# Attention kernel: two PSUM banks for the score tiles and four for the maxima's chunks, in place of three and three

## What is computed

```python
energy = jnp.einsum('bhqd,bhkd->bhqk', q, k)
att = jax.nn.softmax(energy, axis=-1) / D ** 0.5
out = jnp.einsum('bhqk,bhkd->bhqd', att, v)
```

## Time and profile before

| | |
|---|---|
| median of three runs | 2861.51 us (2854.57 to 2863.14) |
| the profiled execution | 2858.09 us, its span 2856.3 us |
| mean granted TensorE clock of the span | 0.976 of full speed |
| matmuls of scores (L385), count and mean | 2048, 419 ns |
| matmuls of chunks (L371), count and mean | 2048, 424 ns |
| exponentials (L463), count and mean | 2048, 607 ns |
| maxima (L502), count and mean | 2048, 681 ns |

### The profile page before, as it was taken

The page is one execution under the profiler, slowest core; times in us unless marked ns, Lnnn a source line. Parts: engine busy times, 40 slices in busy tenths (PEclk is TensorE's granted clock), DMA queues, the critical chain, the costliest instruction groups (busy, mean ns, idle before and its releaser), DMA issues. The chain is left out here.

```text
span 2856.3 us, 61816 instructions
## 1 busy us (share of the span) xinstructions
PE 2659.4 (93%) x22219; PEld 1494.5 (52%) x22273; DVE 2204.9 (77%) x4467; ACT 1844.1 (65%) x3329; POOL 1962.6 (69%) x1571
## 2 busy tenths in 40 slices
PE   7899899999999999999759998999899899959998
PEld 5655466554765547555325554554455455524444
DVE  5778678776888768877677768776878688749998
ACT  4366555665556645566456677667766776658997
POOL 0389724896269952799438987998789799965442
PEclk9999999999999999999979999999999999989999
DMA  6122443223432415223222314322332222252001
GB/s 229 39 58 63 149 123 101 58 69 133 140 94 57 121 70 166 70 62 95 74 78 60 77 32 115 80 57 45 102 79 60 69 76 58 50 205 97 33 29 38
DMA packets 102196, 243.54 MB, mean 85 GB/s; under 512 B 18828, under 2 KB 25108, under 8 KB 101016
## 3 DMA queue, kind: packets, MB, share of 16 engines
q1 hardware_dynamic: 100120, 233.49, 28.9%
q0 software_dynamic: 1792, 6.33, 0.6%
HBM read 99.15 MB, written 38.88 MB: 48 GB/s over the span
## 5 line engine op out<-in xcount | busy, mean ns | idle before, releaser
L502 DVE TENSOR_REDUCE a_mxs<-ps 128x1 f32<-128x512 f32 x2048 | 1268.5, 681 | 256.7 <-PE ps L371 254.3
L463 ACT ACTIVATE a_p<-ps 128x512 f32<-128x512 f32 x2048 | 1042.6, 607 | 202.5 <-PE ps L385 192.2
L342 POOL TENSOR_TENSOR a_sum<-a_p 128x512 f32<-128x512 f32 x768 | 985.3, 1292 | 127.3 <-PE ps L403 104.9
L371 PE MATMUL ps<-a_k,a_q 96*128 96x512 f32 x2048 | 855.0, 424 | 27.9 <-DVE a_mxs L502 24.3
L385 PE MATMUL ps<-a_q,a_k 98*128 98x512 f32 x2048 | 810.4, 419 | 18.6 <-ACT a_p L463 12.4
L347 POOL TENSOR_TENSOR a_sum<-a_sum,a_p 128x512 f32<-128x512 f32 x512 | 663.5, 1296 | 40.1
L403 PE MATMUL ps<-a_sum,a_unit 128*32 128x512 f32 x1536 | 656.4, 598 | 14.8 <-POOL a_sum L347 12.0
L403 PE MATMUL ps<-a_p,xv 128*32 128x512 f32 x3968 | 645.0, 598 | 1.4 <-DVE tok L521 1.4
L371 PEld LDWEIGHTS ps<-a_k,a_q 96*128 96x128 f32 x2048 | 388.9, 190 | 262.8 <-DVE a_mxs L502 108.8
L385 PEld LDWEIGHTS ps<-a_q,a_k 98*128 98x128 f32 x2048 | 384.2, 189 | 256.2 <-ACT a_p L463 161.7
L472 ACT ACTIVATE a_ots<-ps 128x512 f32<-128x512 f32 x256 | 152.6, 598 | 415.9 <-PE ps L403 414.7
(11 more groups left out here) (251 smaller groups left out, 3121.9 us busy)
## 6 DMA issues: line engine op xcount, KB each, us to landing
a_q<-qh SPq DMA_DIRECT2D x256, 128.0 KB, 2.3
a_k<-kh SPq DMA_DIRECT2D x256, 128.0 KB, 2.4
a_q<-ql SPq DMA_DIRECT2D x128, 128.0 KB, 2.3
a_k<-kl SPq DMA_DIRECT2D x128, 128.0 KB, 2.4
x<-a_p SPq DMA_DIRECT2D x64, 256.0 KB, 2.1
a_p<-in_w_fc SPq DMA_DIRECT2D x12, 1024.0 KB, 8.0
kh<-in_x SPq DMA_DIRECT2D x4, 2048.0 KB, 14.3
a_p<-x SPq DMA_DIRECT2D x16, 512.0 KB, 6.3
```

Of the source, the lines that this page charges most:

```text
L342: pair = pool.tensor_tensor(tile, self.key_tile(u, kt), self.key_tile(u, kt + 1), ALU.add)
L371: pe.matmul(self.mx[self.mx_ring[at]], self.q[j][0:96, t * P:(t + 1) * P], self.k[j][0:96, half * HALF:(half + 1) * HALF], start=True, sto ...
L463: act.activation(self.key_tile(u, kt), self.st[self.st_ring[CHUNKS * k + n]], ACT.Exp, scale=self.scale).then_inc(self.s_exp, 1)
L502: dve.reduce_max(self.mxs[:, k % 2, c:c + 1], self.mx[self.mx_ring[CHUNKS * k + c]], axis=AX.X).then_inc(self.s_mxr, 1)
```

## The change

The scores take two banks in turn (tile t takes bank t mod 2). The chunks take four: the first 28 of a batch go round three of them as before (PSUM banks 3 to 5), and from tile 28 on all four are used (PSUM banks 2 to 5). The distance `back` is then 2 for every score. For a chunk it is 4, apart from the start of a batch, where it is 3, for the first tile 1, and for tile 28 it is 32; the credit of the chunks grows for that. No instruction is added or taken away, and the order on each engine is the same.

```diff
-def ring(at):
-
-    return [t % 3 if t < at else (t - (2 if t == at else 1)) % 3 for t in range(H * CHUNKS)]
+EARLY_CHUNKS = 2 * (CHUNKS - 2)
+
+
+def chunk_ring():
+
+    return [(t + 2) % 3 + 1 if t < EARLY_CHUNKS else t % 4 for t in range(H * CHUNKS)]
...
-    MX_CREDIT = 4
+    MX_CREDIT = 32
...
-        self.st_ring, self.mx_ring = ring(CHUNKS + 14), ring(2 * CHUNKS + 10)
+        self.st_ring, self.mx_ring = [t % 2 for t in range(H * CHUNKS)], chunk_ring()
...
-        self.st = [ps[:, n, :] for n in range(3)]
-        self.mx = [ps[:, 3 + n, :] for n in range(3)]
+        self.st = [ps[:, n, :] for n in range(2)]
+        self.mx = [ps[:, 2 + n, :] for n in range(4)]
```

## The result

The changed kernel takes 3043.26 us (median of four runs, 3037.19 to 3047.8), the kernel before 2859.69 us in the same comparison (2854.57 to 2863.14). The ratio is 1.0648, 95% interval 1.0626 to 1.0669: slower by 6.5%. The prediction was 3062 us, in a range of 3020 to 3110. The profiled execution took 3037.19 us with a span of 3035.4, which is 179.1 us more than the span of before.

A forecast was written before the change was run, and what follows sets the result against it. TensorE's sequence was taken to set the pace, with ScalarE the clock inside a stretch. 227 stretches x 0.88 = 200 us, all else booked at 0: 2858 + 200 = 3058 for the profiled execution, 3062 for the median, range 3020 to 3110.

The forecast's parts named there:

- The turn: Scores on two banks: one bank's turn takes 1.19 us, 0.595 a score against 0.49, adding 0.88 us a stretch.
- ScalarE is the clock inside a stretch of before: Stretches of the kernel before: exponentials, one every 0.49 us, set the pace of 3.14 to 3.18 us.
- The count: Stretches that lose: 29.5 a batch, 236 in eight batches, less nine in layer 1; 227 x 0.88 = 200 us.
- the bursts: TensorE's work behind each stretch: hides none of the loss, comes later and stays as long as before.
- the wait for maxima: TensorE's lone 0.8 us wait in a pair of heads: no gain from the fourth chunk bank, 0 booked, bound 51 us.
- The start of a batch: Scores 0 to 13 of head 0, held by maxima: 7.75 us now, 7.6 with two banks, so no loss.
- The tails: Last two heads: three stretches without chunks lose the same 0.88 us; those with products in three layer 1 batches lose nothing.
- GpSimd's waits: Batch ends, where TensorE waits for GpSimd up to 1.51 us: longer stretches remove its backlog; 0 booked, bound 12 us.
- Partly paid back: Rival: slower, but the turn is nearer 1.08 us or waits for GpSimd and maxima shrink; 2974 to 3020 us, 11%.
- Not slower: Rival: maxima are the true clock, scores lose nothing, waits come back; 2810 us, at most 2729; 2%, plus 1% within 0.3%.
- The clock's fall: Rival: TensorE's clock falls; 43 us in five batches' last two heads (3105), another 550 if in the body; 4%.
- the rule of the Trainium skill: Clock in the loop: cycling through PSUM banks can idle TensorE so often that its clock falls and rises repeatedly, costing far more.

The follow-up runs named there:

- two_three: Scores on two banks as in the changed kernel, but chunks kept on three and one bank unused: 3042.92 us, ratio 1.0642 to the kernel before.
- half_dose: Kernel before with two score banks only in tiles 0 to 133 of each batch, three after, chunks on three: 2955.21 us, ratio 1.0333.
- half_exp_two: Changed kernel with each exponential over the first 256 of 512 columns only: 2886.46 us, ratio 1.0092 to the kernel before.
- half_max_three: Kernel before with each chunk's maximum over its first 256 columns only: 2836.17 us, ratio 0.9920.
- half_max_two: Changed kernel with each chunk's maximum over its first 256 columns only: 3038.17 us, ratio 1.0632 to the kernel before.
- tail_dose: Kernel before with two score banks only from tile 210 of each batch on, chunks on three: 2877.47 us, ratio 1.0068.
- ring_early: Kernel before with the irregular place of the score ring moved from tile 30 to tile 4: 2860.87 us over 12 runs, ratio 1.0007.

## Why the prediction was right, and where it was off

**The turn.** The term that decides was the score's two-bank turn of 1.19 us, taken from tile 32 of the trace before. It measured 1.18 to 1.19. The stretch was predicted at 4.04 us and took 4.02 to 4.06 in the stretches of heads 1 to 12 of every batch. That `two_three` equals the changed kernel, that `half_dose` has half the loss, and that the stretch follows the exponential's length in `half_exp_two` shows this step from three sides. What was wrong beside it is the sentence that ScalarE is the clock inside a stretch of before. Short exponentials left that stretch at 3.14 us; one kind is held by both readers, the other almost wholly by TensorE's own starts. It did no harm, since the sum took the stretches of before as measured.

**The count.** 24.5 full stretches a batch lie in the body: 196 x 0.88 = 172 us. The bodies grew by 162.9. The 9.6 us between are in the bursts, which I had said would keep their length. From the last score of a stretch to the first after the burst it was 1848.18 - 1845.07 = 3.11 us before and is 3.05 after, since the last chunk starts 0.24 behind the last score in place of 0.30. The last score of before, at 1845.07, is in the earlier trace rows; behind it come, before and then after (there with the score):

```profile
1845.37 0.39 PE L371 MATMUL ps<-a_k,a_q 96*128 96x512 f32 x1
...
1848.18 0.40 PE L385 MATMUL ps<-a_q,a_k 98*128 98x512 f32 x1
```

```profile
1991.57 0.40 PE L386 MATMUL ps<-a_q,a_k 98*128 98x512 f32 x1
1991.81 0.39 PE L372 MATMUL ps<-a_k,a_q 96*128 96x512 f32 x1
...
1994.62 0.40 PE L386 MATMUL ps<-a_q,a_k 98*128 98x512 f32 x1
```

The shorter bursts are worth 0.19 us a pair (27.66 + 4 x 0.88 = 31.18 against 30.99), some 10 us in all, and `two_three` shows that slower scores gave them back and not the fourth bank. Neither reader alone holds a burst: this one has a median of 3.12 us before, 3.09 with short exponentials, 3.11 with short maxima and 3.04 with both short. What came back isn't the wait for maxima that I had bounded by 51 us and booked at 0. Booking that at 0 was right. The wait is at the weight load of the first chunk behind a burst, and behind the burst before it the same 0.84 us are put down to nothing that the profile shows ("issue"):

```profile
1841.56 0.19 PEld L371 LDWEIGHTS ps<-a_k,a_q 96*128 96x128 f32 x1 [0.84 <-issue]
...
1847.84 0.19 PEld L371 LDWEIGHTS ps<-a_k,a_q 96*128 96x128 f32 x1 [0.84 <-DVE a_mxs L502]
```

The weight load is idle there while the values run, with or without maxima. It is still 0.8 us once a pair in the changed kernel, where I had said that loads for chunks would hardly wait for maxima; in the whole span these waits went from 108.8 us to 85.1.

**The start of a batch** was booked at 0: 7.75 us before, 7.74 after in layer 0. Right there; in layer 1 it went from 8.40 to 8.56 in three batches and from 11.22 to 12.31 in one, 1.6 us in all. The reason is shown as well for layer 0: with short maxima it takes 6.3 us on three score banks (`half_max_three`) and still 7.74 on two (`half_max_two`), so the scores' own turn takes over there, at 7.74 and not at the 7.6 of my sum.

**The tails.** I had 27 us for them and nothing for GpSimd's waits, which I had bounded by 12. Tails and batch changes together came to 34.5 - 14.9 - 3.3 = 16.3. The waits for GpSimd fell by 10.7 us, and `tail_dose` shows that this is bought and paid for in the tail. That accounts for 10.7 of the 14.9 us between batches; what the rest is isn't shown. Within the tails I booked too little, 27 us for 34.5. In the three layer-1 batches with products between the scores, the stretches without chunks were booked at nothing, and two of the three grew from 4.17 to 4.86 and from 4.44 to 4.93, 1.2 us a batch, although two scores of before stood 1.34 us apart. I had looked at one such distance and not at all of them. Most of what remains is in the last batch, whose tail grew by 7.3 us; its clock fell (below).

**The rivals.** "Partly paid back" described something real, about 20 us of returns, but its main term, a turn of 1.08, didn't happen. "Not slower", with the maxima as the clock, is excluded by `half_max_two` for the changed kernel. The clock's fall didn't happen in the loop: 1.00 in the pair, with TensorE idle a little in each turn, so the rule of the Trainium skill that I had set against the row ("TensorE: Matmul & The Clock Gate", section "A second HAM failure mode: psum-queue depth-cycling") isn't borne out there. In the tails it did, in small pieces. The same five tails (batches 0, 1, 2, 3 and 7) had a clock of 1.00, 0.95, 1.00, 1.00, 1.00 before, and after:

```profile
323.00:361.30 38.30, 35.34 (x322) 14.29 (x320) 24.75 (x52) 24.51 (x47) 33.52 (x26) 0.96 0.15 56
689.80:729.70 39.90, 36.91 (x322) 14.57 (x320) 25.31 (x52) 24.47 (x47) 34.12 (x27) 0.91 0.15 55
1058.00:1096.20 38.20, 35.21 (x322) 14.29 (x320) 24.75 (x52) 24.44 (x47) 33.41 (x26) 0.96 0.15 57
...
2667.40:2706.90 39.50, 36.50 (x321) 14.86 (x320) 15.28 (x36) 24.46 (x47) 32.14 (x27) 0.91 0.42 155
```

Batch 3 has the 38.20 us and 0.96 of batch 2. With 0.91 batch 1 took 1.7 us more than they. That is the size of this effect, not the 43 us of my rival.

## What to carry to other kernels

How many banks a producer needs follows from one sum: the turn of a bank is the lag to the next matmul, the time from its start to the reader's start, and the reader's duration (here 0.05 + 0.54 + 0.60 us), and the tiles come no closer together than the turn divided by the banks. Do it for each reader, compare it with the reader's own pace (0.49 us for an exponential, 0.60 for a maximum) and with that of the matmuls, and give a bank only where the turn comes out longest. Both readers here need three. With that, one kind of stretch is 0.1 us over TensorE's own 3.04 and the other about 0.01 over its own 3.16; with two for either of them the kernel loses 6%. The sum was tried with two readers of one kernel only. An irregular place in a ring is worth finding before anything is changed, since it shows the price of the shorter distance.

## What was not expected of the hardware

Exponentials of 0.38 us in place of 0.60 left one kind of stretch on three banks at 3.14 us, and short maxima left it at 3.12; only both together gave 3.04. Two readers of different pace (0.49 and 0.60 us a tile) can hold the same stretch, and leaving out half the work of one alone tells nothing of the other.

Each additional interruption of the full-array matmuls by a round of column-tiled ones cost 0.32 us in TensorE's starts, and 0.25 us net on three banks (28.66 against 27.66 us a pair), where the readers catch up a little during it.

A gain of 4 us inside the batches (`ring_early`) didn't show in the total over 12 runs, in which the mean granted clock had a median of 0.974 in place of 0.977. A run's clock and its time go together closely enough here that small gains should be compared at an equal clock.
